# Four graph layers on one core: the mean subtracted by ScalarE in three norms, and a new order of the blocks

## The chip, the cores and the metric

The kernel runs on one core of a Trainium2 chip. The metric is the time of one execution on the device in microseconds (us), from three runs: 1487.61, 1487.95 and 1488.96, median 1487.95. A separate execution was taken by the hardware profiler; its page and its trace are what is read here. The core has five engines that run side by side: TensorE (PE in the profile; its weight loads stand as PEld), VectorE (DVE), ScalarE (ACT), GpSimd (POOL) and SyncE (SP), which issues the DMA transfers. Each works through its own list of instructions in the order in which they are written and waits at semaphores for the others.

## The reference

128 graphs of 128 nodes with 256 features pass through four layers. Each layer is wrapped in the same way: a layer norm without gain, a ReLU, the layer, and the sum with the layer's input.

```python
for layer in (L0, L1, L2, L3):
    h = jnp.maximum(_layernorm(x, axis=-1), 0.0)   # (x - mean) / sqrt(var + 1e-5), then ReLU
    x = x + layer(h, adj)

L0: out = D^-1 H B^-1 H^T (h W1^T) + b1;  relu;  layer norm with gain and bias;  the same convolution with W2;  + h
L1: e = leaky_relu(Wh a1 + (Wh a2)^T);  softmax over axis 1 where adj > 0.5;  elu(attention @ Wh)
L2: alpha = adj * exp(leaky_relu(s_j + s_i + ab));  rows divided by their sums -> T;  relu(X Wk0 + T X Wk1 + T T X Wk2 + biases)
L3: q, k, v from h;  w = softmax over nodes of sum(q k^T * adj);  w * v
```

All is float32. H is the pattern of the nonzero entries of adj.

## The kernel before

The 128 graphs are worked in 32 groups of four (G = 4). The main loop is a pipeline over groups, and in one round five groups are at different places: the methods and flags of `Round` name them. `next` is group i+1 (first norm, incidence matrices, the smoothed input yT of the first layer), `front` is group i (rest of the first layer, and the attention layer L1), `mid` is group i-1 (L2), `late` is group i-2 (first half of L3) and `tail` is group i-3 (the weights of L3 and the output). Rounds 0 to 3 and the last four are written out, those between are a hardware loop; the list is the same, without the blocks of groups that don't exist.

Products in the weight layers are done three times with operands split into a high and a low part of a shorter format (`split`, names ending in hi and lo): ScalarE makes the high part as it copies out of PSUM, VectorE or GpSimd the low part as the difference. Products of the graphs' own matrices are in full float32 and appear as two records each in the trace.

The order of the work is written out by hand in the `body` function of each engine (L732 TensorE, L961 ScalarE, L1175 GpSimd, L1580 VectorE, L297 SP). A block is a small function; the name says the group, for instance `front_w1(r, hc)`: one 512-wide product block of the first layer, `mid_h2` the transposes of L2's normed input, `mid_p10` and `mid_p2` its weight products, `mid_b2` the spread of a column, `mid_ap` and `mid_az` the products with the transition matrix, `front_w2`, `front_w2_low` and `front_sums` the second weight product of the first layer with the sums for its norm, `front_c2` the second convolution, `front_h1`, `front_wh`, `front_b1` and `front_att` those of the attention layer, `late_h3`, `late_vqk`, `late_ak` those of L3, `tail_row` and `tail_turn` two small transposes of L3's softmax, and `next_s`, `next_d`, `next_y` the preparation of the next group.

The eight PSUM banks are shared by a table (`BANK`, L236) that gives each block its bank. Before a block writes its bank, TensorE waits until the earlier block's readers are done; these waits are written in each block function.

A layer norm has three parts. VectorE takes mean and variance (`bn_stats` L1329, `bn_aggr` L1333) and subtracts the mean into `h` (L1347, in `centred`); TensorE transposes `h`; GpSimd makes 1/sqrt(var + eps) with a power (`rsqrt` L1083 and L1085), and ScalarE applies it later, as a scale in the copies out of PSUM of what is made from `h`. The ReLU is done by ScalarE in the copy of the transposed `h` (L881, L885, L949). The three later norms (layers L1, L2, L3) call `centred` for all four graphs of a group in one go: `front_ln1`, `mid_ln2`, `late_ln3`. The first norm is different: ScalarE does it in one instruction (`norm_x` L918) with a bias that GpSimd makes.

The attention layer ends with an ELU in three steps: VectorE `elu_low` (L1412), ScalarE `elu_exp` (L945), VectorE `elu_high` (L1419). In the kernel before, these stand at the start of the next round's lists, ahead of `mid_ln2`, while TensorE does the four blocks `front_w1` of the next group; `mid_h2` follows on TensorE. `front_penalty` (L1378, the mask `pen`) reads adj_f, and SP loads the next adj_f only after it.

Of the kernel before, what the change touches and what calls it, by code (L numbers as in the profile page):

```python
# [20 lines left out]
class Round:  # L21

    def __init__(self, i, groups, G, steady=False):
        self.i, self.G, self.total, self.steady = i, G, groups * G, steady

        def has(n):
            return steady or 0 <= n < groups

        self.has = lambda d: has(i + d)

        self.has_next, self.has_front, self.has_mid = has(i + 1), has(i), has(i - 1)
        self.has_late, self.has_tail = has(i - 2), has(i - 3)  # L40

    def _value(self, n, k):
        v = n * self.G + k
        if self.steady:
            return v
        return None if v <= 0 else min(v, self.total)

    def group(self, d, k):
        return self._value(self.i + d, k)

    def before(self):
        return Round(self.i - 1, self.total // self.G, self.G, self.steady)

    def next(self, k):
        return self._value(self.i + 1, k)

    def front(self, k):
        return self._value(self.i, k)

    def mid(self, k):  # L60
        return self._value(self.i - 1, k)

    def late(self, k):
        return self._value(self.i - 2, k)

    def tail(self, k):
        return self._value(self.i - 3, k)
# [12 lines left out]
def gnn_stack(nc, x, adjT, w1T, w2T, cols, rows, l1_w, l2_wv, l2_wk, wvT, wqkT, out):  # L80
# [7 lines left out]
    FIRST_STEADY = 4  # L88
# [13 lines left out]
    with ExitStack() as ctx:  # L102
# [42 lines left out]
        rs = sb("rs", 5, G)  # L145
        h0 = sb("h0", G, D)
# [47 lines left out]
        def stage(buffer, at, dims, *sizes):  # L194
# [3 lines left out]
            for v in sizes:  # L198
# [27 lines left out]
        c2_ready x1_ready st1 ag1 h1_ready var1 rs1_ready  # L226
        h1T_ready h1T_copied h1T_lo wh_ready wh_kept wh12_ready b1_spread q_ready lz lr_ready pT_ready rz_ready pT_scaled
        att_ready el_ready ea_ready x2_ready
        st2 ag2 h2_ready var2 rs2_ready h2T_ready h2T_copied h2T_lo p2_ready p2_copied sij_ready sjc_a sjc_ready b2_spread zb_ready zb5_ready eb_ready al_ready
        p10_ready p10_copied ap_ready rsum_a rsum_ready z1_ready p0b_ready az_ready vb_ready relu_ready x3_ready x3_moved  # L230
        st3 ag3 h3_ready var3 rs3_ready h3T_ready h3T_copied h3T_lo vqk_ready vqk_copied ak_ready qak_ready w_ready
# [19 lines left out]
        def rounds(eng, body, first=None):  # L251

            if first:
                first(Round(-1, GROUPS, G))
            for i in range(FIRST_STEADY):
# [3 lines left out]
            for i in range(GROUPS - 1, GROUPS + 3):  # L259
                body(Round(i, GROUPS, G))  # L260
# [10 lines left out]
        def _(sp):  # L271
# [24 lines left out]

            def body(r):  # L297
                if r.has_next:
                    if r.steady or r.i >= 0:

                        wait(sp, S["pen_ready"], r.front(G))
                        wait(sp, S["binc_ready"], r.front(G))
                        sp.dma_start(adj_f[:], group(adjT, r.i + 1)).then_inc(S["adj_f_loaded"], 16)
                        wait(sp, S["h0_ready"], r.front(G))
                        wait(sp, S["xb_ready"], r.front(G))
                        sp.dma_start(x_in[:], group(x, r.i + 1)).then_inc(S["x_loaded"], 16)
                if r.has_tail:
                    wait(sp, S["x4_ready"], r.tail(G))
                    sp.dma_start(group(out, r.i - 3), x4[:]).then_inc(S["stored"], 16)
                if r.has_mid:  # L310

                    wait(sp, S["al_ready"], r.mid(G))
                    wait(sp, S["ak_ready"], r.late(G))
                    sp.dma_start(adj_l[:], adj_m[:]).then_inc(S["adj_l_loaded"], 16)
                    sp.wait_ge(S["adj_l_loaded"], r.loads(r.i - 1))
                if r.has_front:
                    sp.dma_start(adj_m[:], group(adjT, r.i)).then_inc(S["adj_m_loaded"], 16)

            rounds(sp, body)
# [4 lines left out]
        def _(pe):  # L324
# [46 lines left out]
            def first_rows(r):  # L371

                pe.wait_ge(S["rows_loaded"], 96)
                pe.wait_ge(S["deg_ready"], r.next(G))
                spread_rows(ps[:, 5, :], raw_rows[:, 0:2 * D]).then_inc(S["a_spread"], 1)

            def second_rows(r):

                pe.wait_ge(S["yT_lo"], r.front(G))
                pe.wait_ge(S["w2_centred"], HC)  # L380
                spread_rows(ps[:, 6, :], raw_rows[:, 2 * D:4 * D]).then_inc(S["aw_spread"], 1)
                spread_rows(ps[:, 7, 0:D], raw_bk).then_inc(S["aw_spread"], 1)
                spread_rows(ps[:, 7, D:2 * D], raw_bv).then_inc(S["aw_spread"], 1)

            def next_s(r, b):

                if b == 0:
                    wait(pe, S["vqk_copied"], r.late(1))
                    if not r.has_late:
                        wait(pe, S["z_ready"], r.front(G))  # L390
                elif b == 1:
                    wait(pe, S["x1_ready"], r.front(G))
# [9 lines left out]
            def next_d(r):  # L402

                pe.wait_ge(S["deg_ready"], r.next(G))
                wait(pe, S["vb_ready"], r.mid(2))
                if not r.has_mid:
                    wait(pe, S["hT_hi"], r.front(1))
# [4 lines left out]
            def next_y(r, c):  # L412

                if c == 0:
                    wait(pe, S["gt_ready"], r.next(G))
                elif c == 1:
                    wait(pe, S["vqk_copied"], r.late(G))
                    if not r.has_late:
                        wait(pe, S["h1T_lo"], r.front(2))
# [7 lines left out]
            def front_w1(r, hc):  # L427
                if not r.steady and r.i == 0:
                    pe.wait_ge(S["w1_ready"], 1)
                pe.wait_ge(S["yT_copied"], r.front(G))  # L430
                if hc == 0:
                    wait(pe, S["yT_lo"], r.front(2))
                elif hc == 1:
                    wait(pe, S["wh_kept"], r.mid(3))
                    if not r.has_mid:
                        wait(pe, S["deg_ready"], r.front(G))
                elif hc == 2:
                    wait(pe, S["vb_ready"], r.late(G))
                    if not r.has_late:
                        wait(pe, S["wh_kept"], r.mid(2))  # L440
                elif hc == 3:
                    wait(pe, S["wh_kept"], r.mid(1))
# [4 lines left out]
            def late_h3(r, b):  # L447

                if b == 0:
                    wait(pe, S["hT_hi"], r.front(1))  # L450
                    if not r.has_front:
                        wait(pe, S["vb_ready"], r.late(2))
                elif b == 1:
                    wait(pe, S["zb_ready"], r.mid(G))
                    if not r.has_mid:
                        wait(pe, S["h3T_lo"], r.tail(G))
                transposes(S["h3_ready"], r.late, "h3", S["h3T_ready"], b)

            def mid_h2(r, b):

                if b == 0:
                    wait(pe, S["hT_hi"], r.front(2))
                    if not r.has_front:
                        wait(pe, S["wh_kept"], r.mid(3))
# [1264 lines left out]
```

## Time and profile before

| | |
|---|---|
| runs, us | 1487.61, 1487.95, 1488.96 (median 1487.95) |
| profiled execution, span | 1487.0 us, 33717 instructions |
| TensorE busy | 1423.5 us (96%), 8920 matmul records |
| TensorE weight loads | 1263.7 us (85%) |
| VectorE busy | 1206.8 us (81%) |
| ScalarE busy | 978.8 us (66%) |
| GpSimd busy | 949.7 us (64%) |
| HBM | 36.45 MB read, 16.78 MB written |

The span runs from the first to the last instruction of the profiled execution; the time of the runs is measured on other executions and has what lies around the span in it. Busy time of TensorE is wide: its products are pipelined, and the profile gives each record from its entry to a modelled end, so records overlap. The distance from one record's start to the next one's is the better measure of what a product costs. Idle time of an engine that is not the bottleneck costs nothing by itself.

### The profile page before, as it was taken

What the parts mean: (1) busy time and instruction counts of PE and PEld (TensorE: products, weight loads), DVE (VectorE), ACT (ScalarE), POOL (GpSimd) and SP (SyncE); (2) the same over time, 40 slices, a digit from 0 to 9 for tenths busy, and PEclk for the clock granted to TensorE, in tenths of its full rate; (3) what the DMA queues carried; (4) which work ended last, traced back from release to release, by engine and by line L of the source; (5) the groups of instructions that cost most, each with busy time, mean ns of one, the idle gap of its engine ahead of it and who ended that gap; (6) DMA issues with size and microseconds to landing.
All of it is one profiled execution on the core that took longest, in us unless ns stands there. A gap on an engine that the chain in (4) does not pass through costs nothing.

```text
span 1487.0 us, 33717 instructions
## 1 busy us (share of the span) xinstructions
PE 1423.5 (96%) x8920; PEld 1263.7 (85%) x8920; DVE 1206.8 (81%) x4621; ACT 978.8 (66%) x2122; POOL 949.7 (64%) x974
## 2 busy tenths in 40 slices
PE   6799999999999999999999999999999999999975
PEld 5679988889888988988888988888988888988864
DVE  5778888888888888888888888888888888888773
ACT  4456667766667776667776666776666776666754
POOL 4555775666776666676666676675677666677524
PEclk9899999999999999999999999999999999999997
DMA  4001111101111110111110111110111110111001
GB/s 128 22 15 37 37 42 44 49 32 46 35 48 36 49 47 30 35 49 35 49 49 28 42 42 35 49 49 28 45 39 35 49 49 28 49 35 41 23 29 50
DMA packets 75372, 62.01 MB, mean 42 GB/s; under 512 B 3014, under 2 KB 70986, under 8 KB 75339
## 3 DMA queue, kind: packets, MB, share of 16 engines
q1 hardware_dynamic: 75338, 61.63, 12.7%
q8 instruction: 14, 0.23, 0.1%
q14 instruction: 20, 0.16, 0.0%
HBM read 36.45 MB, written 16.78 MB: 36 GB/s over the span
## 4 chain that ended last, share of the span: by engine, by line
PE 75%; ACT 11%; issue 5%; DVE 5%; DMA 1%; POOL 0%; DVEq 0%; ACTq 0%; POOLq 0%; SPq 0%
PE ps L343 35%; PE ps L347 18%; PE ps L328 16%; PE ps L491 4%; ACT wh L851 3%; ACT pT L940 3%; ACT h L918 2%; ACT h2T_hi L881 1%; ACT p L929 1%; PE ps L400 1%; ACT yT_hi L953 1%; DMA x_in<-in_x 1%; DVE stats L1329 1%; DVE h L1347 1%; DVE binc_T L1368 0%
## 5 line engine op out<-in xcount | busy, mean ns | idle before, releaser
L1130 POOL TENSOR_TENSOR x3n<-p,x 128x512 f32<-128x512 f32 x64 | 80.8, 1285 | 252.8 <-ACT p L929 252.8
L851 ACT ACTIVATE p<-ps,rs 128x512 f32<-128x512 f32 (+1 forms) x256 | 138.2, 582 | 106.4 <-PE ps L347 73.7
L1090 POOL TENSOR_TENSOR hT_lo<-hT,hT_hi 128x512 fp32r<-128x512 f32 x126 | 162.8, 1294 | 68.5 <-ACT hT_hi L871 65.4
L1085 POOL TENSOR_TENSOR rs<-var_e,neg_half 128x4 f32<-128x4 f32 x160 | 164.9, 1031 | 23.7
L343 PE MATMUL ps<-wl_hi,h2T_hi 128*128 128x258 f32 (+1 forms) x512 | 148.5, 371 | 7.8 <-ACT h2T_hi L881 7.2
L328 PE MATMUL ps<-p,alT 128*128 128x256 f32 (+1 forms) x512 | 136.9, 390 | 3.3 <-DVE h3T_lo L1239 2.3
L343 PE MATMUL ps<-wl_lo,h2T_hi 128*128 128x258 f32 (+1 forms) x512 | 132.9, 341 | 0.0
L347 PE MATMUL ps<-wl_hi,h2T_lo 128*128 128x258 f32 (+1 forms) x512 | 132.4, 340 | 0.0
L949 ACT ACTIVATE h3T_hi<-ps 128x512 fp32r<-128x512 f32 x64 | 38.0, 594 | 139.0 <-PE ps L491 138.9
L491 PE MATMUL ps<-ident,h 128*128 128x128 f32 x768 | 118.3, 278 | 9.9 <-DVE h L1347 9.4
L491 PEld LDWEIGHTS ps<-ident,h 128*128 128x128 f32 x768 | 92.3, 142 | 32.9 <-issue 10.4
L1347 DVE TENSOR_SCALAR_CACHE_REDUCE h<-x,mv 128x256 f32<-128x256 f32 x256 | 113.6, 463 | 2.3
L1329 DVE BATCH_NORM_STATS2 stats<-x 128x6 f32<-128x256 f32 x256 | 109.2, 426 | 5.5
L1117 POOL TENSOR_TENSOR alT<-zb,adj_m 128x512 f32<-128x512 f32 x32 | 41.1, 1285 | 113.1 <-DVE zb L1438 113.1
L328 PEld LDWEIGHTS ps<-p,alT 128*128 128x128 f32 x512 | 86.4, 190 | 15.7 <-issue 4.8
L343 PEld LDWEIGHTS ps<-wl_hi,h2T_hi 128*128 128x128 f32 x512 | 81.0, 191 | 21.2 <-issue 17.0
L347 PEld LDWEIGHTS ps<-wl_hi,h2T_lo 128*128 128x128 f32 x512 | 88.5, 190 | 11.6
L343 PEld LDWEIGHTS ps<-wl_lo,h2T_hi 128*128 128x128 f32 x512 | 88.4, 190 | 11.3
L851 ACT ACTIVATE vqk<-ps,rs 128x384 f32<-128x384 f32 x128 | 73.9, 577 | 33.8 <-PE ps L347 33.7
L871 ACT ACTIVATE hT<-ps,cols_sb 128x512 f32<-128x512 f32 x128 | 88.1, 689 | 6.6 <-PE ps L347 1.5
L1105 POOL TENSOR_TENSOR x<-x 128x512 f32<-128x512 f32 x64 | 82.0, 1282 | 13.3 <-ACT x L851 13.3
L871 ACT ACTIVATE hT_hi<-ps,cols_sb 128x512 fp32r<-128x512 f32 x128 | 87.6, 684 | 0.1
(178 smaller groups left out, 4476.0 us busy)
## 6 DMA issues: line engine op xcount, KB each, us to landing
x_in<-in_x SPq DMA_DIRECT2D x32, 512.0 KB, 3.9
out_x<-x SPq DMA_DIRECT2D x32, 512.0 KB, 2.9
adj_f<-in_adjT SPq DMA_DIRECT2D x32, 256.0 KB, 2.9
adj_m<-in_adjT SPq DMA_DIRECT2D x32, 256.0 KB, 2.8
adj_l<-adj_m SPq DMA_DIRECT2D x32, 256.0 KB, 2.3
vqk<-in_l_wk SPq DMA_DIRECT2D x3, 256.0 KB, 5.2
x<-in_w2T SPq DMA_DIRECT2D x1, 512.0 KB, 5.1
x<-in_w1T SPq DMA_DIRECT2D x1, 512.0 KB, 5.9
```

The source lines that it names most:

```text
L328: last = pe.matmul(dst, lhsT(c), rhs(c), start=(c == 0), stop=(c == chunks - 1))
L343: pe.matmul(dst, lhsT(a, c), rhs(b, c), start=(a == b == c == 0), stop=False)
L347: last = pe.matmul(dst, lhsT(1 - late, c), rhs(late, c), start=False, stop=(c == chunks - 1))
L491: last = pe.transpose(bank(name, b)[:, ((g % 2) * KC + c) * P:((g % 2) * KC + c + 1) * P], h[:, g, c * P:(c + 1) * P], ident[:])
L851: return act.activation(dst, src, ACT.Copy, scale=scale)
L871: act.activation(dst[:, hc, :], bank("u", hc), ACT.Relu, bias=cols_sb[:, 0, hc:hc + 1]).then_inc(S[ready], 1)
L1085: pool.tensor_tensor(rs[:, layer, :], var_e[:, layer, :], neg_half[:], ALU.pow).then_inc(done, G)
L1090: pool.tensor_tensor(hTs[1][:, hc, :], hT[:, hc, :], hTs[0][:, hc, :], ALU.subtract).then_inc(S["hT_lo"], 1)
L1105: pool.tensor_tensor(x4[:, s], x4[:, s], x3[:, s], ALU.add).then_inc(S["x4_ready"], 2)
L1130: pool.tensor_tensor(x3n[:, s], p0[:, s], x2[:, s], ALU.add).then_inc(S["x3_ready"], 2)
L1329: dve.bn_stats(stats[:, layer, g, :], src[:, g, :]).then_inc(st, 1)
L1347: dve.tensor_scalar(dst[:, g, :], src[:, g, :], mv[:, layer, g, 0:1], None, ALU.subtract, ALU.add, accum_out=unread[:, layer, g:g + 1]).th ...
```

## The change

1. In the three later norms VectorE no longer subtracts the mean. `centred` is replaced by `spread_about`, which takes the statistics of two graphs and makes the negated mean; a new block on ScalarE, `centre`, applies it as the bias of a ReLU into `h`. (`centred` stays in the file and is not called.) The norms are now called for a pair of graphs at a time, `b` = 0 or 1.
2. All five lists are in another order, and the table of PSUM banks is new, with new waits.
3. Some blocks move to another round: the ELU of a group and the first pair of `mid_ln2` stand at the end of the group's own round; `late_ak` moves to the start of the next round; `front_penalty` becomes `next_penalty`, made before the first round for the first group and otherwise one round's list later; `relu_p0` and `add_x3` are done in halves, the second half of `add_x3` in the next round. The first round has a list of its own (`opening`). On SP the load of x stands ahead of that of adj_f.

The new instructions:

```diff
-        BANK = {"u": (0, 4, 3, 2), "y": (0, 7), "s": (4, 5), "d": (0,), "c2": (6, 5), "h1": (7, 1), "wh": (2, 3, 4,
-                5), "b1": (6,), "att": (1, 5), "h2": (4, 3), "p2": (4, 5, 6, 7), "p10": (7, 6, 7, 6), "b2": (5,),
-                "z": (1, 2, 3, 4), "ap": (0, 1, 2, 3), "az": (0, 3), "h3": (0, 5), "vqk": (4, 1, 6, 7), "ak": (6,),
-                "row": (1,), "turn": (7,)}
+        BANK = {"u": (2, 0, 1, 2), "y": (3, 4), "s": (0, 1), "d": (2,), "c2": (1, 2), "h1": (3, 5),
+                "wh": (3, 4, 5, 6), "b1": (7,), "att": (3, 5), "h2": (4, 6), "p2": (4, 5, 6, 7),
+                "p10": (0, 5, 0, 0), "b2": (0,), "z": (1, 2, 3, 4), "ap": (3, 4, 5, 6), "az": (4, 0),
+                "h3": (6, 7), "vqk": (2, 6, 7, 1), "ak": (7,), "row": (2,), "turn": (2,)}
...
+            def centre(layer, src, dst, b, value, ready, done):
+                act.wait_ge(ready, value(2 * b + 2))
+                for g in (2 * b, 2 * b + 1):
+                    act.activation(dst[:, g, :], src[:, g, :], ACT.Relu,
+                                   bias=nmean[:, layer, g:g + 1]).then_inc(done, 1)
...
+            def spread_about(layer, src, b, value, st, ag, done):
+                gs = slice(2 * b, 2 * b + 2)
+                moments(layer, src, (2 * b, 2 * b + 1), value, st, ag)
+                dve.wait_ge(ag, value(2 * b + 2))
+                dve.tensor_scalar(nmean[:, layer, gs], mv[:, layer, gs, 0], -1.0, None, ALU.mult).then_inc(done, 2)
...
+            def relu_p0(r, b):
+                s = slice(2 * b, 2 * b + 2)
+                act.wait_ge(S["vb_ready"], r.mid(2 * b + 2))
+                act.activation(p0[:, s], p0[:, s], ACT.Relu).then_inc(S["relu_ready"], 2)
```

The order of a full round after the change, by block (the group's prefix left out where it is plain; "past" is the round before, "ahead" the one after):

```
TensorE  w1(0 1 2), h2(0), ak of past, w1(3), p2(0), h2(1), p10(0), w2(2), w2(0), p2(1), row, p2(2), p2(3), w2(1),
         w2_low(0), b2, w2(3), w2_low(1 2 3), sums(0-3), p10(1), h3(0), p10(2), c2(0), turn, c2(1), ap(0-3),
         c2(2), c2(3), p10(3), h3(1), h1(0), az(0), s(0), s(1), az(1), vqk(0), h1(1), wh(0), vqk(1), wh(1 2 3),
         d, b1, az(2), az(3), y(0), vqk(2), y(1), vqk(3), att(0-3)
ScalarE  copy_u(0), mid_centre(0), copy_u(1), copy_h2T(0), mid_centre(1), copy_u(2), copy_u(3), copy_h2T(1),
         square(0), late_centre(0), square(1), copy_p10(0), tail_exp, copy_p2(0 1), exp_edges, copy_p2(2),
         copy_p10(1), copy_h3T(0), copy_p2(3), late_centre(1), copy_p10(2), norm_x(0), weigh(0), front_centre(0),
         copy_p10(3), copy_h1T(0), front_centre(1), copy_s(0), copy_h3T(1), copy_h1T(1), weigh(1), copy_s(1),
         copy_vqk(0 1), norm_x(1), relu_p0(0), keep_x3, keep_wh(0 1), copy_yT(0), softmax(0 1), keep_wh(2),
         copy_yT(1), keep_wh(3), copy_vqk(2 3), elu_exp(0), relu_p0(1), elu_exp(1)
VectorE  moments, tail_sum, mid_low(1), penalty of past, tail_max, columns, count, ln3(1), tail_norm, inverse, binc,
         variance, edges, z(0-3), late_low(0), residual(0), tail_out, ln1(0), z1_scale, residual(1), z1(0 1), ln1(1),
         z1(2), front_low(0), z1(3), late_low(1), vb(0 1), front_low(1), degrees, columns, gt, logits, leaky(0 1),
         max(0), vb(2), max(1), y_low(0), weights(0 1), y_low(1), elu_low(0), vb(3), elu_low(1), elu_high(0),
         ln2(0) ahead, elu_high(1), ln2(1) ahead, mid_low(0) ahead, ln3(0) ahead, tail_weights ahead
GpSimd   res0(0 1), x3(1) of past, lo(0), rsqrt 2, lo(1 2 3), squares, join, rsqrt 0, rsqrt 4, mask_edges, shift_x,
         add_bias(0), xb(0), rsqrt 3, rsqrt 1, x4(0), add_bias(1), xb(1), x4(1), x3(0)
SP       load x, adj_m to adj_l (past), load adj_m (past), load adj_f, store out
```

The opening round's list on VectorE: two low parts, `first_dots`, count, `second_dots`, variance, inverse, binc, z(0-3), moments, then the norm of L1 by pairs and the rest. On GpSimd the low parts of the wide weights stand after the scale of L1's norm instead of before the scale of the next group's first norm.

## Rows read from the trace of the kernel before

**Rows 1.** Busy time by window: stretch, its length, busy us (records) per engine, clock, DMA.
```profile
752.30:796.60 44.30, 43.90 (x281) 39.32 (x280) 37.25 (x146) 30.43 (x67) 29.60 (x31) 1.00 0.13 41
```
**Rows 2.** TensorE's timeline (start, us, operation): first w1 product of rounds 2 and 31.
```profile
102.73 0.80 PE L343 MATMUL ps<-yT_hi,w_hi 128*128 128x512 f32 x2
...
1387.08 0.81 PE L343 MATMUL ps<-yT_hi,w_hi 128*128 128x512 f32 x2
```
**Rows 3.** TensorE's timeline in round 18: records that follow without a wait.
```profile
811.42 0.63 PE L343 MATMUL ps<-yT_hi,w_lo 128*128 128x512 f32 x2
...
820.06 0.40 PE L347 MATMUL ps<-wl_hi,h2T_lo 128*128 128x258 f32 x2
820.30 0.40 PE L343 MATMUL ps<-wl_hi,h2T_hi 128*128 128x258 f32 x2
...
837.33 0.52 PE L347 MATMUL ps<-wl_hi,h3T_lo 128*128 128x384 f32 x2
837.68 1.02 PE L328 MATMUL ps<-z,gt 128*128 128x256 f32 x4
...
841.43 1.03 PE L328 MATMUL ps<-p,alT 128*128 128x256 f32 x4
842.30 0.61 PE L328 MATMUL ps<-binc_T,inc_T 128*128 128x129 f32 x4
842.74 0.60 PE L491 MATMUL ps<-ident,h 128*128 128x128 f32 x4
```
**Rows 4.** The same round: transposes h2 and the product behind them.
```profile
816.56 1.18 PE L491 MATMUL ps<-ident,h 128*128 128x128 f32 x8
817.99 0.71 PE L343 MATMUL ps<-wl_hi,h2T_hi 128*128 128x512 f32 x2 [0.26 <-ACT h2T_hi L881]
```
**Rows 5.** Groups of instructions by form, 310 to 1200 us: count, busy us, mean ns.
```profile
L1347 DVE TENSOR_SCALAR_CACHE_REDUCE h<-x,mv 128x256 f32<-128x256 f32 x163 | 72.3, 462 | 1.5
L1329 DVE BATCH_NORM_STATS2 stats<-x 128x6 f32<-128x256 f32 x160 | 68.2, 426 | 3.4
L1333 DVE BATCH_NORM_AGGREGATE mv<-stats 128x2 f32<-128x6 f32 x321 | 53.2, 168 | 0.0
L1412 DVE SCALAR_TENSOR_TENSOR el<-ps,x 128x512 f32<-128x512 f32 x40 | 27.3, 681 | 0.0
L918 ACT ACTIVATE h<-x_in,nmr,rs 128x256 f32<-128x256 f32 x80 | 43.4, 596 | 0.0
L851 ACT ACTIVATE x<-vqk,wcol 128x256 f32<-128x256 f32 x80 | 34.1, 497 | 16.5 <-DVE wcol L1544 16.5
L945 ACT ACTIVATE ps<-ps 128x512 f32<-128x512 f32 x40 | 23.3, 582 | 24.4 <-DVE el L1412 24.4
```
**Rows 6.** TensorE's timeline in the drain: h2, then h3 and ak of the last group.
```profile
1434.60 2.41 PE L491 MATMUL ps<-ident,h 128*128 128x128 f32 x8 [4.41 <-DVE h L1347]
...
1466.35 2.40 PE L491 MATMUL ps<-ident,h 128*128 128x128 f32 x8 [4.36 <-DVE h L1347]
...
1475.27 1.10 PE L328 MATMUL ps<-vqk,adj_l 128*128 128x64 f32 x8 [0.73 <-ACT vqk L851]
```
**Rows 7.** The opening: VectorE's timeline, and TensorE's last sums (33.48).
```profile
32.59 0.29 DVE L1356 TENSOR_SCALAR_CACHE_REDUCE inc_T<-adj_f 128x128 f32<-128x128 f32 x1 [5.07 <-DMA adj_f<-in_adjT]
...
33.48 0.28 PE L328 MATMUL ps<-mean_w,sq 128*128 128x1 f32 x2
...
36.06 0.42 DVE L1276 CUSTOM_DVE_ANT_0 zb<-alT,ps 128x256 f32<-128x256 f32 x1
...
40.88 0.16 DVE L1457 COPY hst<-ps 128x4 f32<-128x4 f32 x1
...
43.21 1.66 DVE L1468 SCALAR_TENSOR_TENSOR z<-ps,rs,bw 128x256 f32<-128x256 f32 x4 [0.33 <-POOL rs L1085]
```
**Rows 8.** VectorE's timeline in a steady round: pen, and the count behind the load.
```profile
774.70 0.42 DVE L1378 TENSOR_SCALAR pen<-adj_f 128x512 f32<-128x512 f32 x1
...
778.22 0.29 DVE L1356 TENSOR_SCALAR_CACHE_REDUCE inc_T<-adj_f 128x128 f32<-128x128 f32 x1 [1.68 <-DMA adj_f<-in_adjT]
```

More of the change, by code:

```diff
@@ L249, in four, with rounds @@
             return ps[:, b[0]:b[3] + 1:b[1] - b[0]]
-        def rounds(eng, body, first=None):
+        def rounds(eng, body, opening=None, first=None):
             if first:
                 first(Round(-1, GROUPS, G))
-            for i in range(FIRST_STEADY):
+            if opening:
+                opening(Round(0, GROUPS, G))
+            for i in range(1 if opening else 0, FIRST_STEADY):
                 body(Round(i, GROUPS, G))
@@ L295, in _, with load_adj, load_x @@
             sp.dma_start(raw_l3[:, :, D:], chunked(wqkT)).then_inc(S["l3_loaded"], 16)
+            def load_adj(r):
+                wait(sp, S["pen_ready"], r.front(G))
+                sp.dma_start(adj_f[:], group(adjT, r.i + 1)).then_inc(S["adj_f_loaded"], 16)
+            def load_x(r):
+                wait(sp, S["h0_ready"], r.front(G))
+                if not r.steady and r.i in (0, 1, 2, 3,):
+                    wait(sp, S["xb_ready"], r.front(G))
+                sp.dma_start(x_in[:], group(x, r.i + 1)).then_inc(S["x_loaded"], 16)
@@ new lines, in store, with hand_adj, load_mask @@
+            def store(r):
+                sp.wait_ge(S["x4_ready"], r.tail(G))
+                sp.dma_start(group(out, r.i - 3), x4[:]).then_inc(S["stored"], 16)
+            def hand_adj(r):
+                wait(sp, S["ak_ready"], r.late(G))
+                sp.dma_start(adj_l[:], adj_m[:]).then_inc(S["adj_l_loaded"], 16)
+            def load_mask(r):
+                if r.steady or r.i > 0:
+                    sp.wait_ge(S["adj_l_loaded"], r.loads(r.i - 1))
+                sp.dma_start(adj_m[:], group(adjT, r.i)).then_inc(S["adj_m_loaded"], 16)
@@ L297, in body @@
             def body(r):
+                past = r.later(-1)
                 if r.has_next:
[L299 to L306, printed above, removed]
@@ L307, in body @@
-                if r.has_tail:
[L308 to L317, printed above, removed]
@@ L429, in front_w1 @@
                     pe.wait_ge(S["w1_ready"], 1)
-                pe.wait_ge(S["yT_copied"], r.front(G))
[L431 to L442, printed above, removed]
+                if hc == 1:
+                    wait(pe, S["vb_ready"], r.late(G))
+                elif hc == 2:
+                    wait(pe, S["vqk_copied"], r.tail(G))
+                elif hc == 3:
+                    if not r.steady and r.i == 0:
+                        wait(pe, S["hT_hi"], r.front(1))
+                pe.wait_ge(S["yT_copied"], r.front(G))
                 split_product(bank("u", hc), lambda a, c: w1s[a][:, c, hc * P:(hc + 1) * P],
@@ L854, in copy_vqk @@
                 if g == 0:
-                    wait(act, S["vw_ready"], r.tail(2 if r.has_mid else G))
+                    if not r.steady and r.i in (GROUPS, GROUPS + 1,):
+                        wait(act, S["vw_ready"], r.tail(2))
                 act.wait_ge(S["rs3_ready"], r.late(G))
@@ L1073, in first @@
                 l1_hi()
-            rounds(act, body, first)
+            rounds(act, body, opening, first)
         @block.gpsimd
@@ L1227, in _ @@
             constants()
-            rounds(pool, body, first)
+            rounds(pool, body, opening, first)
         @block.vector
```

844 lines of the change are left out of this document (457 added, 387 removed).

## The prediction

> **What bounds the kernel now.** I read the busy table by window first, then TensorE's timeline over one round, then who ended its waits, then the opening and the drain. In a steady stretch of 44.30 us TensorE is busy 43.90, VectorE 37.25, ScalarE 30.43, GpSimd 29.60, and the granted clock is 1.00, its level of 2.4 GHz [rows 1]. TensorE sets the pace, but a busy share of 99% does not say that its work fills the round. For that I count the work at the spacing that it has where nothing holds it, and compare with the length of a round.
>
> The round: the first product of the first layer (block w1) starts at 102.73 and 29 rounds later at 1387.08 [rows 2]: 1284.35 / 29 = 44.29 us.
>
> The work of a round, in matmul records, spaced as [rows 3] show: 48 of 512 columns (w1, p10) at 0.234 us ((816.56 - 811.42) / 22; the second end is in [rows 4]) = 11.2; 96 of 258 columns (p2, w2, wh) at 0.12 = 11.5; 24 of 384 columns (vqk) at 0.175 ((837.68 - 837.33) / 2) = 4.2; 32 of 256 or 257 columns (ap, c2, az, att: two records to a product) at 0.217 (0.87 for four) = 6.9; 36 transposes and 40 short products, at 0.11 (0.44 for four) = 8.4; the two small transposes of the tail, about 0.4. Sum 42.6 us. So 44.29 - 42.6 = 1.7 us of each round is waiting, spread over several places, and 1.7 us is all that an order of blocks can win there. The largest wait shows in [rows 4]: the eight transposes h2 should take 0.87, of which the next block usually absorbs 0.08, but p10 starts 1.43 after them: 0.64 lost, ended by ScalarE's copy h2T_hi. It follows from the order: h2(1) (0.44) alone stands between h2(0) and the product that needs its copy. 0.44 + 0.64 = 1.08, less a 512-wide ScalarE instruction of 0.58 [rows 5], leaves 0.5 for two handovers. I use 0.35 from TensorE to a reader and 0.15 for any other handover (estimates from this).
>
> **The change, part by part.** I sum against the profiled execution's span, 1487.0; the median of the runs is 1487.95, and I add the difference back at the end.
>
> *VectorE* loses 12 subtractions a round (three norms, four graphs) of 0.462 and gets 6 negations of two columns and 6 fillers; the nearest small operation is the aggregate of 0.168 [rows 5], so at most 12 x 0.168. Net between -5.5 and -3.5 us of 37.25. Alone this is worth nothing: VectorE has 7 us idle in a round. Taken: 0.
>
> *ScalarE* gets 12 activations of 128x256 with a bias. The trace has none of that kind; nearest are x4's with a scale (0.497) and h0's with scale and bias (0.596) [rows 5]. I take 0.5 (range 0.41 to 0.6): +6.0, and one more instruction as relu_p0 is halved. 30.4 + 6.2 = 36.6 us of a round of 43: hidden as a load, by 6 us of idle time, but it runs in written order, so what matters is who stands behind a waiting activation.
>
> *The order.* I lay the new round along TensorE, with 0 where w1(0) starts, and ask at each block whether its operand is there.
> - Round boundary: h2(0) now has three w1 blocks ahead, 18 x 0.234 = 4.2, not four. Its chain is shorter too: only the first pair is needed. att(1) ends at -0.87; elu_low(0) from -0.5 (0.68), exp (0.58), elu_high(0) behind elu_low(1), done at 1.7; two statistics of 0.426, aggregates, filler and negation, 3.1; ScalarE, through with copy_u(0) at 2.9, two centrings, 4.2. Wait 0 to 0.1. In the drain of before, where nothing stands between, the old chain takes 4.41 from att to h2 [rows 6].
> - p10(0) stands behind w1(3), p2(0) and h2(1) now, so the copy of h2T is long there: the 0.64 goes. Next late is p2(0), which needs h2T_lo at about 6.8, with TensorE there at 6.9.
> - From the last sums to c2(0) stand p10(1), h3(0), p10(2): 1.40 + 0.44 + 1.40 = 3.24. Variance, GpSimd's power and the first z take 0.35 + 2.33 (40.88 to 43.21) + 0.48 + 0.15 = 3.3 [rows 7]. Wait 0.1.
> - w2(1) waits for the tail's exponent, about 0.15 spare; wh(3) for copy_vqk(1), 0.05 spare; b1 for its columns, 0.1 late.
> - y(0) waits for keep_wh(0). ScalarE, from the end of vqk(1): 0.35, the rest of copy_vqk(0) and copy_vqk(1) about 1.0, norm_x(1) 1.1, half of relu_p0 0.55, keep_x3 1.0 (twice the 512-wide one), keep_wh(0) 0.47, 0.15 = 4.6; on TensorE wh(1 to 3), d, b1, az(2, 3) = 3.9. Behind the slower figures 0.3 to 0.6 late. Behind y(0) stand vqk(2), y(1), vqk(3), 3.0 us, which cover the softmax.
>
> These waits sum to 0.5 to 0.9; seven more places have under 0.2 to spare, and I read handovers to 0.1. Taken: 0.9. Round 42.6 + 0.9 = 43.5 us. Below, 42.8, if nearly all waits go; above, 44.3, if as much waiting comes back; beyond that only through a rival. 29 x (44.29 - 43.5) = -23 us.
>
> *SP's queue.* It issues the same five transfers a round. The load of adj_f now stands behind pen at about 11.5, and behind adj_l and adj_m, which go out at 5.8 and 8.1 when ak of the round is done. Before, counting starts 3.1 us after pen ends (775.12 to 778.22 in [rows 8]); in the new order VectorE reaches it 3.3 after. Taken: 0.
>
> *The opening.* In before, adj_f is loaded only once pen is made, at 27.5; VectorE waits the 5.07 us before 32.59 for it, and the first variance stands behind that, behind the moments and the second dots: it starts at 40.88, while the sums that it needs were done at 33.76, and z starts at 43.21 [rows 7]. Now pen is made before the first round, so by my count the load goes out near 15; the moments stand behind z; second_dots (4.8 us, 36.06 to 40.87) ends near 32.4. Variance at 34.1, z at 36.4: -6.8. GpSimd's weight remainders move behind the first norm's scale; they are next needed a round later. Taken -6.5; between 0 (adj_f comes no sooner) and -7.5.
>
> *The drain.* The last round has no next group: -0.8 like the others. In before, h3 of the last group starts at 1466.35, when both halves of x3 and all four statistics allow, and ak at 1475.27 [rows 6]. Halved relu_p0 and x3 let h3(0) and two vqk blocks run before the second half arrives, and the exponents of round 32 come earlier: I count about 5 us off the start of ak; the tail's chain behind it (11.7) is unchanged. Taken -5; 0 to -8.
>
> Sum: 1487.0 - 23 - 6.5 - 0.8 - 5 = 1451.7; with the 0.95 to the median, 1452.6. Predicted 1452.5.
>
> A rule speaks against the first half of the change: the Trainium skill, "Perfetto Trace Analysis", section "Optimizing Scalar/DVE Operations", says that moving work from VectorE to ScalarE may pay when VectorE is saturated; it adds that where neither engine is saturated, breaking instructions up can let work complete sooner. VectorE is at 84% here [rows 1], so by that rule the moved subtraction earns nothing by itself, and the sum above gives it nothing either; the halves (norm, relu_p0) are what its second sentence speaks of. No row of before shows a moved subtraction, so whether the rule holds here is open. The case in which nothing but the ends is won is the first rival below.
>
> **Rivals.**
> 1. *The waits only move.* The new order has as many tight places as the old; rounds stay at 44.3 and only opening and drain shrink: 1487.95 - 6.5 - 5 = 1476.5. For it: a dozen places with under 0.2 us to spare, each a different engine's lateness. Against: the two largest old waits had a block too few in front, and the new places have the blocks. This is what the rule above would make of it, if the halves bring nothing.
> 2. *ScalarE's order.* A centring costs 0.6, with its handover 0.7, and the four that precede keep_wh(0) without idle time behind them push y(0) and then keep_wh(3) before att(3): 1 us more waiting, a round of 44.5, 1488 + 6 - 11.5 = 1482. For it: ScalarE's load rises by a fifth. Against: copy_p10(3) and the exponents are waits that absorb most of it.
> 3. *Slower: adj_f lands late.* Counting stands ahead of the third norm's second half, binc and the variance on VectorE, so a late landing delays z and c2(0) directly, and with them TensorE. Spare: 0.2 at the load, 0.3 at the variance. It is slower than before once a round loses 0.8 + 11.5/29 = 1.2 us more, so from a landing 4.9 us after pen instead of 3.1. In the opening the wait was 5.07 [rows 7]; with that much every round, 1.5 more late than break-even: 1488 + 44 = 1532. With 0.5 beyond break-even, 1502. Against: 1.68 is the wait in the steady row [rows 8], at 3.1 after pen.
>
> **How the numbers follow.** Forecast 0.64 (own range 1436 to 1468: rounds of 43.0 to 43.9, ends by their bounds); rival 1 0.17; rival 2 0.10; rival 3 0.06; 0.03 for rounds at the floor (29 x 1.5 + 12.3 = -56, 1432). Range 1434 to 1479, which takes in the forecast and rival 1 and leaves out rival 3, half of rival 2 and the floor. A measurement of this kernel can tell about 0.2%, 3 us, from no change. Faster 0.88 (forecast, rival 1, floor and 0.04 of rival 2); the same 0.04 (rival 2 where ScalarE costs some 0.2 us a round more than priced); slower 0.08 (rival 3 and the far end of rival 2).
>
> **What would show it.** Starts of w1 43.5 us apart, not 44.3; no wait before p10 on h2T_hi; the longest TensorE waits on keep_wh (before y) and small ones at c2; ScalarE's busy time near 36 in a round, VectorE's near 33; the first z near 36.4; ak of the last group about 40 us after the end of the last att, not 45. The prediction is wrong if rounds are not shorter than 44, if TensorE waits for a centred h in every round, or if VectorE waits for adj_f over 2 us.

## The result, and the profile after

The changed kernel takes 1477.83 us (median of 4 runs, 1476.98 to 1479.37) beside 1488.06 for the kernel before on the same chip: ratio 0.993, 95% interval [0.9917, 0.9942]. On a second chip it was 1477.16 beside 1487.70, 0.993 [0.9913, 0.9946]. It gained 10 us where 35.5 were forecast. The time lies inside the range, and close to rival 1 (1476.5), but is not made as rival 1 had it. Against the profiled execution of before:

| part | before | forecast | after |
|---|---|---|---|
| 29 steady rounds, each | 44.29 | 43.5 | 43.93 |
| first w1 to the second round's w1 | 45.1 | 38.6 | 47.4 |
| second round | 41.3 | | 41.6 |
| last w1 to the end | 99.9 | 94.1 | 96.6 |

The length of a round is the distance of two w1 starts, as in [rows 2]: (1379.61 - 105.71) / 29 = 43.93. TensorE's timeline, start, length, operation:

```profile
105.71 0.82 PE L352 MATMUL ps<-yT_hi,w_hi 128*128 128x512 f32 x2
...
1379.61 0.81 PE L352 MATMUL ps<-yT_hi,w_hi 128*128 128x512 f32 x2
```

Busy time by window, the columns of [rows 1]: ScalarE has gone from 30.43 to 34.95 us in a stretch of 44, VectorE from 37.25 to 35.77, not to 33:

```profile
752.00:796.00 44.00, 43.20 (x282) 39.11 (x280) 35.77 (x132) 34.95 (x79) 29.98 (x31) 1.00 0.13 42
```

The waits of TensorE between 105 and 1379 us (total, times, longest) are nearly all one, and it is at none of the places that the prediction listed: att waits, in each of 29 rounds, for VectorE's scaled softmax weights pT. The wait in front of p10 in [rows 4] is gone.

```profile
PE ps L337 <- DVE pT L1531: 22.3, 29, 0.8
```

That is 0.77 us a round. By spacing it is 0.95: the record ahead of att is followed after 1.12 us instead of 0.17. Without it the round would be 43.0, so nothing else of size waits. VectorE's timeline from the logits to the weights shows why they are late: the leaky step (L1509, the leaky ReLU of the attention's logits, two instructions) takes 2.08 us.

```profile
757.44 1.12 DVE L1503 SCALAR_TENSOR_TENSOR q<-ps,wh,pen 128x128 f32<-128x128 f32 x4
758.48 2.08 DVE L1509 SCALAR_TENSOR_TENSOR pT<-q 128x256 f32<-128x256 f32 x2
760.48 0.41 DVE L1515 TENSOR_REDUCE qmax<-pT 128x2 f32<-128x256 f32 x1
760.81 0.47 DVE L1495 SCALAR_TENSOR_TENSOR p<-ps,rsum,p 128x256 f32<-128x256 f32 x1
...
761.53 0.68 DVE L1248 TENSOR_TENSOR yT_lo<-ps,yT_hi 128x512 fp32r<-128x512 f32 x1
762.13 0.15 DVE L1526 RECIPROCAL rz<-zsum 128x2 f32<-128x2 f32 x1
762.31 0.34 DVE L1531 TENSOR_SCALAR_CACHE_REDUCE pT<-pT,rz 128x128 f32<-128x128 f32 x1
```

GpSimd's timeline of the same microseconds: it adds x3n and then, with no pause, the residual (res0 = xb + h0) of the next group, from 757.57 to 761.70.

```profile
757.57 1.27 POOL L1126 TENSOR_TENSOR x3n<-p,x 128x512 f32<-128x512 f32 x1 [1.56 <-ACT x L842]
758.80 2.90 POOL L1132 TENSOR_TENSOR res<-xb,h 128x512 f32<-128x512 f32 x2
```

The groups of instructions (count, busy us, mean ns, idle before) of the changed kernel, then the same three of the kernel before, where GpSimd does the residual among the squares and is idle beside the leaky step:

```profile
L1509 DVE SCALAR_TENSOR_TENSOR pT<-q 128x256 f32<-128x256 f32 x64 | 64.3, 1042 | 0.0
...
L1385 DVE TENSOR_SCALAR pen<-adj_f 128x512 f32<-128x512 f32 x32 | 24.2, 757 | 0.0
...
L1132 POOL TENSOR_TENSOR res<-xb,h 128x512 f32<-128x512 f32 x64 | 91.9, 1456 | 0.0
```

```profile
L1502 DVE SCALAR_TENSOR_TENSOR pT<-q 128x256 f32<-128x256 f32 x64 | 26.6, 416 | 0.1
...
L1378 DVE TENSOR_SCALAR pen<-adj_f 128x512 f32<-128x512 f32 x32 | 13.8, 432 | 0.1
...
L1136 POOL TENSOR_TENSOR res<-xb,h 128x512 f32<-128x512 f32 x64 | 83.2, 1301 | 0.0
```

In the kernel before, the leaky step falls into the 8.06 us that GpSimd waits ahead of x3n, from 757.45 on. VectorE's and GpSimd's timelines:

```profile
761.44 0.41 DVE L1502 SCALAR_TENSOR_TENSOR pT<-q 128x256 f32<-128x256 f32 x1
...
765.51 2.53 POOL L1130 TENSOR_TENSOR x3n<-p,x 128x512 f32<-128x512 f32 x2 [8.06 <-ACT p L929]
```

The same instruction, 1042 ns instead of 416: 2 x 0.63 = 1.25 us more in the chain that ends the round.

### The profile page after: what moved, and what is told of

It reads as the page before. It is cut to its first block, busy times and chain, and to the rows that moved or that the text cites. A ratio compares the mean times of both kernels' runs of the same rounds, so it can differ in the third digit from the quotient of the medians.

```text
span 1476.2 us, 32698 instructions
## 1 busy us (share of the span) xinstructions
PE 1409.3 (95%) x8920; PEld 1268.5 (86%) x8920; DVE 1155.9 (78%) x4237; ACT 1125.7 (76%) x2538; POOL 963.6 (65%) x974
## 4 chain that ended last, share of the span: by engine, by line
PE 82%; DVE 8%; issue 7%; ACT 1%; DMA 0%; DVEq 0%; POOL 0%; POOLq 0%; ACTq 0%; SPq 0%
PE ps L352 36%; PE ps L337 20%; PE ps L356 18%; PE ps L459 6%; DVE q L1503 2%; PE ps L405 2%; DVE p L1495 1%; DVE qmax L1515 1%; DVE pT L1531 1%; DVE yT_lo L1248 1%; DVE pT L1509 1%; DVE stats L1339 0%; DVE rz L1526 0%; PE ps L619 0%; DMA x_in<-in_x 0%
## 5 line engine op out<-in xcount | busy, mean ns | idle before, releaser
L782 ACT ACTIVATE p<-ps,rs 128x512 f32<-128x512 f32 (+1 forms) x256 | 148.1, 592 | 122.4 <-PE ps L356 93.9
L891 ACT ACTIVATE h<-x,nmean 128x256 f32<-128x256 f32 x256 | 116.4, 504 | 23.5 <-DVE nmean L1358 23.4
L337 PE MATMUL ps<-p,alT 128*128 128x256 f32 (+1 forms) x512 | 131.8, 380 | 0.0
L459 PE MATMUL ps<-ident,h 128*128 128x128 f32 x768 | 112.3, 275 | 6.1 <-ACT h L891 5.1
L337 PEld LDWEIGHTS ps<-p,alT 128*128 128x128 f32 x512 | 89.9, 190 | 8.7
L1091 POOL TENSOR_TENSOR sq<-sq 128x512 f32<-128x512 f32 x64 | 83.0, 1298 | 17.5 <-ACT sq L794 14.4
L337 PE MATMUL ps<-wh,pT 128*128 128x256 f32 x256 | 64.7, 397 | 29.1 <-DVE pT L1531 24.9
L1132 POOL TENSOR_TENSOR res<-xb,h 128x512 f32<-128x512 f32 x64 | 91.9, 1456 | 0.0
L1064 POOL TENSOR_SCALAR var_e<-mv 128x4 f32<-128x4 f32 x128 | 31.4, 245 | 90.2 <-DVE mv L1344 87.7
L352 PE MATMUL ps<-yT_hi,w_hi 128*128 128x512 f32 x256 | 89.4, 430 | 0.8 <-ACT yT_hi L881 0.8
```

The source lines that it names most:

```text
L337: last = pe.matmul(dst, lhsT(c), rhs(c), start=(c == 0), stop=(c == chunks - 1))
L352: pe.matmul(dst, lhsT(a, c), rhs(b, c), start=(a == b == c == 0), stop=False)
L459: last = pe.transpose(bank(name, b)[:, ((g % 2) * KC + c) * P:((g % 2) * KC + c + 1) * P], h[:, g, c * P:(c + 1) * P], ident[:])
L782: return act.activation(dst, src, ACT.Copy, scale=scale)
L891: act.activation(dst[:, g, :], src[:, g, :], ACT.Relu, bias=nmean[:, layer, g:g + 1]).then_inc(done, 1)
L1091: pool.tensor_tensor(sq[:, 2 * k, :], sq[:, 2 * k, :], sq[:, 2 * k + 1, :], ALU.add).then_inc(S["sq_half"], G // 2)
```

## The experiments

Lengths of rounds are worked out as above, from each trace's w1 starts. Ratios are to the kernel before on the same chip, with the 95% interval.

**1. The residual back behind the squares.**

```diff
 GpSimd, body:
-    add_res0(r, 0); add_res0(r, 1)       # first in the round, ahead of add_x3
     ...
     join_squares(r)
+    add_res0(r, 0); add_res0(r, 1)
     next_scale(r)
```

> The changed kernel with one edit: GpSimd makes the residual (two additions of 128x512) behind the joined squares, where it waits 3.5 us for VectorE's variance, and no longer ahead of x3n, where it runs beside VectorE's leaky step. Theory A (the collision): the leaky step has both inputs in SBUF and takes 1042 ns beside GpSimd's additions, 416 in the kernel before; without them it takes about 0.42 again, the softmax chain on VectorE ends 1.25 us sooner, the wait of att (0.8 to 0.95 us a round) goes, rounds fall from 43.93 to about 43.0, the time to 1478 - 29 x 0.93 - 1 = 1450. Theory B (the order on VectorE: vb and the low half of yT stand inside the softmax chain, and the leaky step is slow for another reason): leaky stays near 1.04, rounds stay at 43.9, 1478. Theory C (ScalarE's added work is late): rounds stay at 43.9 as well, with the wait on ScalarE's exponents.

Measured: 1443.38, ratio 0.969 [0.9669, 0.971]; rounds of (1344.80 - 100.77) / 29 = 42.90. The leaky step fell to 517 ns and the wait of att is gone; one wait is left in the same stretch of TensorE's list. Its groups, then its waits:

```profile
L1508 DVE SCALAR_TENSOR_TENSOR pT<-q 128x256 f32<-128x256 f32 x64 | 30.7, 517 | 0.0
...
L1132 POOL TENSOR_TENSOR res<-xb,h 128x512 f32<-128x512 f32 x64 | 80.8, 1283 | 0.0
```

```profile
PE ps L352 <- DVE h2T_lo L1251: 0.5, 1, 0.5
```

So one edit of two calls is worth 1.03 us a round and 34 us in all, 30 of them in the 29 rounds, and theories B and C fall. Why 517 and not 416: the addition x3n (to 739.26) still reaches into the first leaky step. Its timelines, GpSimd and VectorE:

```profile
737.99 1.27 POOL L1126 TENSOR_TENSOR x3n<-p,x 128x512 f32<-128x512 f32 x1 [1.54 <-ACT x L842]
...
738.90 0.97 DVE L1508 SCALAR_TENSOR_TENSOR pT<-q 128x256 f32<-128x256 f32 x2
```

**2. One work item less inside the softmax chain.** The order on VectorE as the rival cause.

```diff
 VectorE, body:
     front_max(r, 0)
-    mid_vb(r, 2)
     front_max(r, 1)
     y_low(r, 0); front_weights(r, 0); front_weights(r, 1)
+    mid_vb(r, 2)
```

> The changed kernel with one edit: on VectorE the attention update vb of the third graph (0.47 us) stands behind the softmax weights instead of between the two maxima. A: the chain is 0.4 us shorter and the rest of the wait stays, rounds 43.55, 1467; leaky stays at 1.04. B: the order is the cause, so nearly all of the wait goes, rounds 43.1, 1454. C: no change, 1478.

Measured: 1482.62, 0.9945 [0.9925, 0.9965], rounds 44.09, leaky 1041 ns. The expectation of theory A was wrong here as well. The wait of att fell to 15.8 us in 28 rounds, but vb now stands behind the weights, ahead of the ELU and the statistics of h2, and h2 and h3 are late instead: the weight loads of their transposes wait for the centred h, which they do not in the steady rounds of the changed kernel. In one round compared record by record TensorE loses 0.3 us more at h2 and 0.15 more at h3, and 0.2 less at att. Moving work along VectorE's list gave nothing here; making an item of it shorter (experiment 1) did.

```profile
PE ps L337 <- DVE pT L1531: 15.8, 28, 0.6
...
PEld ps L459 <- ACT h L891: 15.6, 56, 0.4
```

**3. One SBUF input.** Whether it is the two SBUF inputs of the leaky step that meet GpSimd.

```diff
-    scalar_tensor_tensor(pT[:, s, :], q[:, s, :], SLOPE, q[:, s, :], mult, max)
+    scalar_tensor_tensor(pT[:, s, :], d_ps,       SLOPE, q[:, s, :], mult, max)   # d_ps: a PSUM bank
```

> The changed kernel with the residual left where it is and one operand of the leaky step read from a PSUM bank instead of SBUF: same operation, same shape, one SBUF input; the slope's branch takes another operand, so that part of the computation is changed. Theory A in its narrow form (only a VectorE instruction with both inputs in SBUF waits for GpSimd's addition): the step takes 0.45 to 0.48 though the additions run beside it, rounds 43.0, about 0.971 of the kernel before. Rival (whatever VectorE does in that stretch is slowed, or the additions are in the way by their order): the step stays above 0.8, 0.99.

Measured: 1445.13, 0.9704 [0.9687, 0.9722], rounds 42.87. The residual stays where the change put it; the groups show the leaky step at 413 ns beside it, and the addition at 1289:

```profile
L1510 DVE SCALAR_TENSOR_TENSOR pT<-ps,q 128x256 f32<-128x256 f32 x64 | 23.9, 413 | 0.0
...
L1132 POOL TENSOR_TENSOR res<-xb,h 128x512 f32<-128x512 f32 x64 | 81.1, 1289 | 0.0
```

That is the cause: a VectorE instruction with both inputs in SBUF is held up by a GpSimd addition on SBUF, one with an input in PSUM is not. By the Trainium skill, "SBUF — State Buffer", section "Who interferes with whom", a VectorE instruction with two SBUF inputs contends with a GpSimd instruction that reads SBUF, and one with at most one SBUF input, outside the two-port modes, does not; 1042 against 413 ns agrees. The same section counts `tensor_scalar` among those that can contend, except in the form that also writes its accumulator; pen agrees (757 against 432 ns; it now runs beside GpSimd's additions of the squares, and no run moved it), and so does the old subtraction with an accumulator (L1347 in [rows 5]): in the kernel before, those of the norms L1 and L2 that ran beside an addition of GpSimd took 460 ns, the others 477.

**4. The same collision in the old order.**

```diff
 GpSimd, body of the kernel before (round 0 keeps its own):
-    add_res0(r, 0); add_squares(r, 0); add_res0(r, 1); add_squares(r, 1)
+    add_squares(r, 0); add_squares(r, 1)
     ...
     add_xb(r, 1)
+    add_res0 for the next group, 0 and 1
     add_x3(r, 0); add_x3(r, 1)
```

> The kernel before with one edit: GpSimd makes the residual of the next group right ahead of x3n, where it idles 8 us in each round, beside VectorE's softmax chain, and no longer among the squares. Theory A (collision): one of the two leaky steps of a round now runs beside an addition and takes 1 to 1.5 us instead of 0.42, the chain is 0.6 to 1.1 late with next to nothing to spare, rounds 44.8 to 45.2, 1503 to 1515. Theory B (the leaky step is slow in the changed kernel for another reason than GpSimd): leaky stays at 0.42, 1488, or a little less since the squares are free of the residual.

Measured: 1501.23, 1.0094 [1.0077, 1.0111], rounds 44.71. The leaky step has a mean of 683, 0.53 us a round more, a little less than expected, and the round grew by 0.42.

```profile
L1508 DVE SCALAR_TENSOR_TENSOR pT<-q 128x256 f32<-128x256 f32 x64 | 43.7, 683 | 0.1
```

**5. The mean subtracted on VectorE in the new order**, with the collision, and without it (together with experiment 1).

```diff
-    spread_about(1, x1, b, r.front, S["st1"], S["ag1"], S["nm1_ready"])
+    centred(1, x1, h, b, r.front, S["st1"], S["ag1"], S["h1_ready"])     # norms 2 and 3 alike
     ScalarE: front_centre, mid_centre, late_centre are not called; three waits for buffers more
```

> The changed kernel with the mean subtracted on VectorE again in all three later norms (two more waits for buffers): the new order without the offload. A: VectorE has 12 subtractions of 0.46 a round again and 6 negations fewer, about 39.7 us of work in a round of 44, and the centred h comes later in each norm; the new order depends on the offload: rounds of 44.5 to 45.5, 1495 to 1525. C (ScalarE's added work is what is late): ScalarE falls to 30 us a round and rounds shrink to about 43.4, 1463. If the offload neither helps nor hurts: 1478 within 3.

Measured: 1505.82, 1.0098 [1.008, 1.0116], rounds 44.80.

> The changed kernel with the residual moved back behind the squares, and the mean subtracted on VectorE again: prices the offload where nothing collides. If VectorE's chain around the end of the round is then what bounds the round (as A says, since that chain from the logits to the statistics of h2 has no idle time), the subtraction costs up to 0.8 us a round there: 43.5 to 44.0, 0.98 to 0.99. If the offload is worth nothing once the collision is gone: 42.9, 0.969.

Measured: 1470.24, 0.9897 [0.9876, 0.9917], rounds 43.73. With the runs so far this is a square, in us a round (44.29 before):

| | residual beside the leaky step | residual behind the squares |
|---|---|---|
| mean subtracted by VectorE | 44.80 | 43.73 |
| by ScalarE | 43.93 (the change) | 42.90 |

The offload is worth 0.87 and 0.83, the collision costs 1.07 and 1.03: they add up. So the new order by itself, without offload and collision, gives 44.29 - 43.73 = 0.56. The size was as expected for the second kernel, the place was not: no wait of size stands at att or h2. Most of it is at p10(2), which waits until VectorE has read the bank of the edges (zb), and that stands behind the third norm's subtractions: 0.3 to 0.7 us in each of five rounds compared record by record with experiment 1. The waits of TensorE's products and of its weight loads:

```profile
PE ps L352 <- DVE zb L1436: 9.8, 25, 1.0
...
PEld ps L352 <- DVE zb L1436: 16.3, 27, 1.3
PEld ps L352 <- DVE h2T_lo L1237: 7.9, 29, 1.2
```

**6. The offload alone in the old order.**

```diff
 VectorE, old order: in place of four subtractions two negations of a pair's means
 ScalarE, old order:
     copy_u(r, 0); copy_u(r, 1)
+    mid_centre(r, 0)
     copy_u(r, 2)
+    mid_centre(r, 1)
     copy_h2T(r, 0)                       # late_centre and front_centre likewise ahead of their copies
```

> The kernel before, in its old order, with the offload alone: VectorE makes the negated means, ScalarE subtracts, twelve activations of 0.45 us a round placed right ahead of the copies that need them. As the prediction priced it: the subtraction leaves VectorE for nothing there, 0 by itself; 1488 within 4. As the runs in the new order suggest (0.85 to 0.89 us a round): the handover to h2 gets shorter in the old order as well, rounds 43.4 to 43.9, 1462 to 1477. Against both: h2 stands right behind w1 in the old order and ScalarE's four copies of the first layer stand ahead of its centring, so that h2 comes later: rounds 44.8 to 45.5, 1503 to 1523.

Measured: 1529.99, 1.028 [1.0263, 1.0298], rounds 45.52: the third case. h2 waits for the centred h, 0.8 us a round of the 1.23 lost, behind ScalarE's copies of the first layer. Another place for the centring in ScalarE's old list was not tried.

```profile
PE ps L492 <- ACT h L965: 21.6, 27, 0.8
```

**7. The opening, and both edits together.** In the opening, VectorE makes the first low half of yT ahead of the softmax weights; then this with experiment 1; then also the moments of the next x behind the first norm's statistics.

```diff
     front_max(r, 1)
+    y_low(r, 0)
     front_weights(r, 0); front_weights(r, 1)
-    y_low(r, 0)
     y_low(r, 1)
```

> The changed kernel with one edit in the opening alone: VectorE makes the first low half of yT ahead of the softmax weights, not behind them, since the first att block waits for that low half (it reuses its PSUM bank). Theory for the opening: of its 47.4 us (45.0 before), 1.1 is this wait, and another 1 to 1.5 the lower TensorE clock that follows the idle stretch; round 0 takes 45 to 46.3, 1475.5 to 1477. Rival (the opening is long because of the leaky collision and the clock alone): round 0 stays at 47.4, 1478. Steady rounds stay at 43.93 in either.

Measured: 1477.21, 0.9909 [0.9892, 0.9926]: not told apart from the change, though round 0 took 42.9 in its profile; the next round took 43.2 instead of 41.6. Not all of the 4.5 us in round 0 is the edit's: the profile of experiment 2, whose opening has the same lists as the change, shows 45.7 (64.78 - 19.05), with the clock at 1.00 from 28 to 32 us, where the change's own profile has 0.57.

> The changed kernel with the residual moved back behind the squares and, in the opening, the first low half of yT ahead of the softmax weights. If the two are the same microseconds of the opening (either alone brings round 0 to 42.9 from 47.4): the time of the first alone, 0.969 of the kernel before. If they add up: 1.5 to 3 us less, 0.967.

Measured: 1442.66, 0.9702 [0.9686, 0.9718]; the two do not add up. Round 0 takes 41.4, but the next one 41.5 where experiment 1 has 40.2: 82.8 us for both instead of 83.1. Steady rounds take 42.89.

> The kernel with the residual moved back and the low half of yT ahead of the weights, and one more edit in the opening: the moments of the next group's x (1.9 us on VectorE, behind z) move behind the statistics of the first norm. If they delayed the first norm as the trace of the changed kernel suggests (x1 starts 1.1 us behind the product it needs): wh starts 1 us sooner, 0.969 to 0.970, 1441.5; if the norm of the next x becomes late in their place (y needs it): no change, 0.970.

Measured: 1447.06, 0.9719 [0.9703, 0.9736]: no gain. Round 0 took 47.2 in its profile, with the lower clock early on that the change's own profile shows (below), so that this one run doesn't tell what the moved moments cost.

**8. The change itself again**, for its opening.

> The changed kernel itself, unedited, on the chip of the three runs beside it. All theories: 0.993 of the kernel before, rounds of 43.9. Its opening is looked at: if the granted clock falls at 28 to 32 us again, that belongs to the kernel; if not, to one execution.

Measured: 1477.16, 0.993 [0.9913, 0.9946], rounds 43.93, round 0 47.4 again, and the clock fell again (0.50 from 28 to 30 us, 0.76 to 32). By the expectation the fall would belong to the kernel; experiment 2, with the same opening and no fall, speaks against that.

## Why the prediction was wrong

Of the 24.5 us by which the profiled execution missed its forecast, 12.5 are the steady rounds', 8.8 the opening's and 2.5 the drain's.

**The steady round (forecast -0.79, measured -0.36 us).** The cover of the softmax failed; the worth of the offload and the waits taken were wrong too, the other way.

- The step that failed: "Behind y(0) stand vqk(2), y(1), vqk(3), 3.0 us, which cover the softmax." It walked the new order along TensorE, ScalarE, VectorE and SP's queue, but of GpSimd's list it placed the power, the halves of x3 and the weight remainders, not the residual. The residual's move to the front of GpSimd's round stands in the diff, and nothing in the prediction says whose instructions it then runs beside. It made the leaky step 1.25 us longer, and the cover was 0.95 short. Experiments 1, 3 and 4 show this from three sides. Its price in the new order is 1.03 to 1.07 us a round, some 30 us, more than the whole shortfall.
- "*VectorE* ... Alone this is worth nothing ... Taken: 0." In the new order it was worth 0.83 to 0.87 us a round; in the old order, as placed in experiment 6, it cost 1.2. 7 us of idle time did not make it free: the waits of experiment 5 put most of its worth at the edges, ahead of which VectorE's items follow each other without idle time from the count on, a subtraction among them. That this decides it elsewhere too is not shown. The rule of the Trainium skill that the prediction weighed ("Perfetto Trace Analysis", section "Optimizing Scalar/DVE Operations": offload where VectorE is saturated) was read there as 0 too; VectorE was at 37.08 of 43.00 us in experiment 5's second kernel, and the offload paid.
- The order itself gave 0.56, and the floor by my count, 42.6, was near: with no wait of size left the round is 42.9, so 0.3 of waiting where 0.9 was taken. The waits forecast at h2, c2, w2, wh and on keep_wh(0) are not among those of TensorE's products in the profile. (The lateness at y(0) was also summed wrongly: 4.6 less 3.9 is 0.7, not 0.3 to 0.6.)

Without the collision the change gives 1443, 9 us below my forecast; rounds of 42.90 lie just under the 43.0 at which its own range ended.

**The opening (forecast -6.5, measured +2.3).** Pen ahead of the first round does what was said: the load's wait of [rows 7] is gone and z starts 4.1 us sooner, counted from w1, where 6.8 were forecast. What followed was taken to keep its length, and in the changed kernel it grew: that is the step that failed here. Starts, in us from the first w1:

| | before | change | residual moved | both edits |
|---|---|---|---|---|
| z | 26.8 | 22.7 | 21.0 | 21.0 |
| wh | 35.0 | 31.8 | 30.2 | 30.3 |
| b1 | 38.8 | 36.7 | 35.0 | 34.8 |
| att | 43.4 | 44.2 | 41.3 | 39.7 |
| next w1 | 45.1 | 47.4 | 42.9 | 41.4 |

Two things in this table are not the forecast's. The 5.07 us of [rows 7] are of one execution: in experiment 4, where the opening stands as it was up to z, VectorE waits 3.01 us there and z starts at 24.8, so the gain at z is nearer 2 to 4 us than 4 to 6. And one product of 1.05 us stood ahead of the first w1 and stands behind its first block now; TensorE's timelines, the kernel before and the changed one:

```profile
15.33 1.12 PE L369 MATMUL ps<-p,ones 1*128 1x512 f32 x2
```

```profile
18.29 1.12 PE L378 MATMUL ps<-p,ones 1*128 1x512 f32 x2
```

From z to the next w1 it is 18.2 us before and 24.7 after. VectorE and TensorE in the changed kernel's opening:

```profile
55.33 1.09 DVE L1509 SCALAR_TENSOR_TENSOR pT<-q 128x256 f32<-128x256 f32 x1
...
60.90 3.78 PE L337 MATMUL ps<-wh,pT 128*128 128x256 f32 x8 [4.13 <-DVE yT_lo L1248]
```

The leaky steps collide here too (0.42 each in the kernel before). att waits 4.13 us, in the end for the low half of yT: the new table puts the first att into the bank of y(0), and VectorE makes that half only after the weights. And att then runs at the clock's lower level, 1.2 GHz: 3.2 us to the next w1 where it was 1.7. Busy time by window, clock in the column ahead of the last two, the changed kernel and then the kernel before:

```profile
28.00:30.00 2.00, 2.00 (x7) 1.57 (x7) 1.93 (x15) 1.69 (x5) 1.93 (x2) 0.57 0.00 0
40.00:46.00 6.00, 5.81 (x18) 4.63 (x18) 5.76 (x21) 1.29 (x3) 2.44 (x5) 0.55 0.00 0
50.00:52.00 2.00, 2.00 (x11) 2.00 (x11) 0.20 (x1) 0.39 (x1) 2.00 (x3) 0.50 0.01 4
60.00:64.00 4.00, 3.10 (x7) 2.52 (x8) 2.13 (x5) 0.25 (x2) 0.00 (x0) 0.50 0.03 6
```

```profile
28.00:30.00 2.00, 2.00 (x18) 2.00 (x17) 0.00 (x0) 0.14 (x1) 1.86 (x2) 1.00 0.66 184
40.00:46.00 6.00, 2.25 (x5) 1.85 (x6) 4.19 (x26) 0.00 (x0) 4.12 (x5) 0.50 0.00 0
50.00:52.00 2.00, 1.71 (x10) 1.14 (x10) 1.68 (x9) 1.20 (x3) 1.66 (x4) 1.00 0.00 0
58.00:62.00 4.00, 2.68 (x14) 2.20 (x14) 3.53 (x15) 2.61 (x12) 0.00 (x0) 1.00 0.03 8
```

In this opening the kernel before has one stretch at the lower level, the changed kernel four. The prediction counted no clock at all. How the 6.5 us between 18.2 and 24.7 divide is open in part: round 0 takes 47.4 with the collision and the fall of the clock at 28 us, 45.7 with the collision alone (experiment 2), 46.2 with the fall alone (experiment 3) and 42.9 with neither (experiment 1), one profile each but for the first.

**The drain (forecast -5.8, measured -3.3).** TensorE's timeline, the rows that answer to [rows 6]:

```profile
1424.82 1.12 PE L459 MATMUL ps<-ident,h 128*128 128x128 f32 x4 [3.54 <-ACT h L891]
...
1453.69 0.63 PE L459 MATMUL ps<-ident,h 128*128 128x128 f32 x4
...
1457.14 0.99 PE L352 MATMUL ps<-wl_hi,h3T_hi 128*128 128x384 f32 x2
...
1464.46 1.10 PE L337 MATMUL ps<-vqk,adj_l 128*128 128x64 f32 x8 [0.73 <-ACT vqk L782]
```

h2 comes 0.87 us sooner than in [rows 6]. ak starts 43.2 us after the end of att (1464.46 - 1421.28), not 40. "Halved relu_p0 and x3 let h3(0) and two vqk blocks run before the second half arrives" is half right: h3(0) does, 2.7 us ahead, but tail_turn and h3(1) stand ahead of vqk(0) in the list, and vqk(0) has the bank of tail_turn. This was read from the trace and the code; no run tried it.

**What held.** The wait before p10 went; VectorE waits 13.1 us in all for adj_f (59.0 before), 3.5 of it at the very start and at most 0.5 in a round; ScalarE's twelve centrings cost 504 to 527 ns each (0.5 taken) and hide in the new order. Rivals 2 and 3 did not occur. Rival 1's time came out, its mechanism did not: rounds did shrink, and the ends together gave nothing.

## What to carry to other kernels

Walk every engine's moved instructions, those off the path too, and ask beside what each will now run: a VectorE instruction with two SBUF inputs on the path and a GpSimd addition beside it cost this kernel three quarters of its gain. Price an offload by the run of instructions without idle time from which it takes work (here read from the waits at one place), and by what stands ahead of it in the new engine's list (experiment 6), not by busy shares: the offload was worth +0.85 us a round in one order and -1.2 in another.

## What the hardware showed

- Which VectorE instructions GpSimd's additions hold up goes by their form. In the changed kernel VectorE's statistics (427 ns) and its readers of PSUM (473 to 477) have the same length within 6 ns beside them as away from them; the leaky step goes from 416 ns in the kernel before to 1042, and pen from 432 to 757. GpSimd's residual loses less, 1456 against 1283.
- TensorE's clock in the opening differs between executions: between 28 and 32 us it was granted 0.57 (mean of 1.2 and 2.4 GHz) in the profile of the change, and fell in the second one of it and in experiments 3, 4, 6 and the last of 7 too; it stayed at 1.00 in the kernel before and in experiments 1, 2, 5 and the first two of 7. In the new order z follows w1 by 22.7 us with that fall and by 21.0 without. What decides it is open: experiment 2 has the same opening as the change and no fall.
